# Quantised attention output transposed by DMA instead of TensorE, last four FFN tiles transposed by TensorE, all engine orders rewritten

## The reference, cut to what matters

```
x = layernorm(x + attn(x))              # attn: chunked recurrence with decay, W_write, W_read
# ffn, H = 256, I = 704:
xq = fp4_quant_dequant(x)               # per block of 16: scale = max|x|/6; q = grid(x/scale)*scale
gate = xq @ fp4_quant_dequant(w_gate).T
up   = xq @ fp4_quant_dequant(w_up).T
h    = silu(gate) * up
y    = fp4_quant_dequant(h) @ fp4_quant_dequant(w_down).T
out  = layernorm(x + y)
```

## Time and profile before

| | us |
|---|---|
| median of 3 runs | 320.72 (320.18 to 323.29) |
| the profiled execution | 319.53 |
| its span, first to last instruction | 317.8 |
| TensorE busy in the span | 299.8 (94%) |
| VectorE busy | 278.9 (88%) |
| GpSimd busy | 241.5 (76%) |
| ScalarE busy | 223.8 (70%) |

### The profile page before, as it was taken

How to read it: one execution, slowest core, us unless ns; L and a number is a source line. 1 busy time by engine, 2 the same in 40 slices (tenths; PEclk the granted TensorE clock), 3 DMA queues, 4 the chain that set the end, 5 groups by cost and what they waited for, 6 DMA issues and landing times.

```text
span 317.8 us, 6470 instructions
## 1 busy us (share of the span) xinstructions
PE 299.8 (94%) x1911; PEld 271.1 (85%) x1911; DVE 278.9 (88%) x725; ACT 223.8 (70%) x545; POOL 241.5 (76%) x258
## 2 busy tenths in 40 slices
PE   6949999999999989999999999999999999999783
PEld 2939988999899879889999998999999998899682
DVE  4996699969999999999988996989998899998953
ACT  7582986679677488669785886686877758587563
POOL 2897886476968967896978889487998757769671
PEclk9996999999999999999999999999999999999979
DMA  6704011832637446433562269338463273267601
GB/s 223 279 35 134 1 68 34 140 74 86 185 75 121 92 86 144 157 95 98 150 180 75 65 107 198 88 104 151 103 120 84 67 112 84 71 136 130 77 33 66
DMA packets 38722, 34.36 MB, mean 108 GB/s; under 512 B 25760, under 2 KB 31776, under 8 KB 38688
## 3 DMA queue, kind: packets, MB, share of 16 engines
q1 hardware_dynamic: 32064, 22.81, 34.5%
q10 hardware_dynamic: 6624, 11.15, 11.1%
HBM read 22.87 MB, written 5.18 MB: 88 GB/s over the span
## 4 chain that ended last, share of the span: by engine, by line
PE 67%; POOL 9%; issue 7%; DVE 7%; DMA 6%; ACT 3%; SPq 1%; ACTq 0%; POOLq 0%; DVEq 0%
PE ps L2160 15%; PE ps L2161 15%; PE ps L2164 15%; PE ps L2173 5%; PE ps L2174 5%; PE ps L2170 5%; DMA h_gT<-h_g 4%; POOL h_q L504 3%; DMA w_pair<-in_w_attn_dram 2%; PE ps L2224 2%; POOL h_n L485 1%; DVE hqT_lo L1584 1%; PE ps L2269 1%; POOL pr_lo L445 1%; PE ps L2283 1%
## 5 line engine op out<-in xcount | busy, mean ns | idle before, releaser
L2160 PE MATMUL ps<-guT_hi,xqT_hi 128*128 128x512 f32 (+1 forms) x192 | 74.0, 385 | 1.5 <-ACT xqT_hi L822 1.4
L2161 PE MATMUL ps<-guT_lo,xqT_hi 128*128 128x512 f32 (+1 forms) x192 | 72.1, 375 | 0.0
L504 POOL TENSOR_TENSOR h_q<-h_gT,h_sT 128x768 f32<-128x768 bf16 x30 | 51.8, 1731 | 12.3 <-DVE hqT_lo L1584 10.7
L2164 PE MATMUL ps<-guT_hi,xqT_lo 128*128 128x512 f32 (+1 forms) x192 | 56.5, 375 | 0.0
L485 POOL TENSOR_TENSOR h_n<-w_raw,h_rs 128x704 f32<-128x704 f32 x32 | 47.1, 1473 | 9.0 <-DVE h_rs L1414 8.9
L2160 PEld LDWEIGHTS ps<-guT_hi,xqT_hi 128*128 128x128 f32 x192 | 36.1, 188 | 6.8 <-ACT xqT_hi L822 1.7
L445 POOL TENSOR_TENSOR pr_lo<-pr,pr_hi 128x512 fp32r<-128x512 f32 (+3 forms) x32 | 28.5, 901 | 16.8 <-ACT pr_hi L791 16.8
L2164 PEld LDWEIGHTS ps<-guT_hi,xqT_lo 128*128 128x128 f32 x192 | 35.5, 188 | 6.0 <-DVE xqT_lo L1521 0.2
L2161 PEld LDWEIGHTS ps<-guT_lo,xqT_hi 128*128 128x128 f32 x192 | 36.1, 188 | 4.5
L2160 PE MATMUL ps<-dnT_hi,hqT_hi 128*128 128x256 f32 x160 | 39.6, 283 | 0.0
L2161 PE MATMUL ps<-dnT_lo,hqT_hi 128*128 128x256 f32 x160 | 39.5, 283 | 0.0
(11 more groups left out here) (130 smaller groups left out, 852.1 us busy)
## 6 DMA issues: line engine op xcount, KB each, us to landing
h_sT<-h_scales_dram SPq DMA_DIRECT2D x30, 384.0 KB
out_dram<-wq_gu ACTq DMA_DIRECT2D x31, 128.0 KB, 1.8
xs<-in_x_rows_dram ACTq DMA_DIRECT2D x7, 512.0 KB, 4.6
x_full<-in_xt_rows_dram ACTq DMA_DIRECT2D x6, 512.0 KB, 3.7
w_raw<-in_w_ffn_dram SPq DMA_DIRECT2D x6, 352.0 KB, 6.0
h_scales_dram<-h_s SPq DMA_DIRECT2D x30, 32.0 KB, 2.6
w_pair<-in_w_attn_dram SPq DMA_DIRECT2D x1, 512.0 KB, 5.1
x_full<-in_xt_rows_dram SPq DMA_DIRECT2D x1, 512.0 KB, 3.5
```

Source lines behind the costliest of these rows:

```text
L504: nc.gpsimd.tensor_tensor(h_q[:, p, :], h_gT[:, p, :, :].rearrange("p c t -> p (c t)"), h_sT[:, p, :], ALU.mult).then_inc(h_quant, 1)
L2160: nc.tensor.matmul(dst, lh, rh, start=(first and i == 0), stop=False)
L2161: nc.tensor.matmul(dst, lh, rl, start=False, stop=False)
L2164: last = nc.tensor.matmul(dst, ll, rh, start=False, stop=(end and i == len(terms) - 1))
```

## The change

- `xq_transpose` goes. `x_scale_rows` takes its place on TensorE: one small transpose of the scales (48 rows) per half batch. New are `copy_x_scales` on ScalarE and, on SyncE's queue, `write_x_scales`, `spread_x_scales` (256 KB) and `turn_x_grid` (a DMA transpose of 128x512 bf16), 16 of each.
- `x_dequant` becomes `x_spread`, which waits for both landings; `x_g` becomes bf16; `xq_round` and `xq_rest` read `x_q` from SBUF and no longer from PSUM.
- `x_divisors` writes the scales in the permuted layout that the transposed form wants.
- FFN tiles 28 and 29 leave the DMA path and go like 30 and 31: `h_dequant`, two `h_transpose` groups, `h_repeat`, `h_round`, `h_rest`. Their two sets of three DMAs and their `h_scale_rows` go.
- All tables of banks and all five orders are new. Between the two orders `gate_up(0)` moves behind both `reads` of batch 1, all `scores` and `values` of batch 2 and the weight fills 6 to 8; at the end `down(26)` moves ahead of `gate_up(31)`.

```diff
+            def write_x_scales(n, u):
+                sp.wait_ge(xs_copied, 2 * n + u + 1)
+                sp.dma_start(x_scales_dram[2 * n + u], x_s[:, u, :]).then_inc(xs_written[u], 16)
+            def spread_x_scales(n, u):
+                sp.wait_ge(xs_written[u], 16 * n + 16)
+                if n >= 1:
+                    sp.wait_ge(x_quant, 2 * n + u - 1)
+                sp.dma_start(x_sT[:, u, :], over_rows(x_scales_dram[2 * n + u], XC, 2 * DK)).then_inc(xs_landed[u], 16)
+            def turn_x_grid(n, u):
+                sp.wait_ge(x_grid, 2 * n + u + 1)
+                if n >= 1:
+                    sp.wait_ge(x_quant, 2 * n + u - 1)
+                sp.dma_start_transpose(x_gT[:, u, :, :], x_g[:, u, :]).then_inc(xg_turned[u], 16)
...
-            def x_dequant(n, u):
-                pool.wait_ge(x_grid, 2 * n + u + 1)
+            def x_spread(n, u):
+                pool.wait_ge(xs_landed[u], 16 * n + 16)
+                pool.wait_ge(xg_turned[u], 16 * n + 16)
                 if n >= 1:
-                    pool.wait_ge(xqT_filled, 2 * n + u - 1)
-                nc.gpsimd.tensor_tensor(
-                    blocks(x_q[:, 2 * u:2 * u + 2, :].rearrange("p i d -> p (i d)")), blocks(x_g[:, u, :]),
-                    per_block(x_ns[:, u, 0:2 * XB], 2 * XB), ALU.mult).then_inc(x_quant, 1)
+                    pool.wait_ge(xqT_lo_ready, 2 * n + u - 1)
+                nc.gpsimd.tensor_tensor(x_q[:, u, :], x_gT[:, u, :, :].rearrange("p c t -> p (c t)"), x_sT[:, u, :],
+                                        ALU.mult).then_inc(x_quant, 1)
...
+            def copy_x_scales(n, u):
+                act.wait_ge(xs_filled, 2 * n + u + 1)
+                if n >= 1:
+                    act.wait_ge(xs_written[u], 16 * n)
+                nc.scalar.copy(x_s[:, u, :], ps[0:XHELD, xs_at[n][u], 0:P]).then_inc(xs_copied, 1)
...
             def x_to_grid(n, u):
+                if n >= 1:
+                    dve.wait_ge(xg_turned[u], 16 * n)
                 to_grid(x_g[:, u, :], ps[:, x_sq_at[n][u], :], x_y[:, u, :], x_magic, x_grid, 2 * n + u + 1)
...
             def xq_rest(n, u):
                 dve.wait_ge(xqT_hi_ready, 2 * n + u + 1)
-                c = slice(D * u, D * (u + 1))
-                nc.vector.tensor_tensor(xqT_lo[:, :, c], ps[:, xq_at[n][u], :].rearrange("p (c t) -> p c t", c=DK),
-                                        xqT_hi[:, :, c].bitcast(F32), ALU.subtract).then_inc(xqT_lo_ready, 1)
+                c = slice(2 * u, 2 * u + 2)
+                nc.vector.tensor_tensor(xqT_lo[:, c, :, :].rearrange("p i c t -> p (i c t)"), x_q[:, u, :],
+                                        xqT_hi[:, c, :, :].rearrange("p i c t -> p (i c t)").bitcast(F32),
+                                        ALU.subtract).then_inc(xqT_lo_ready, 1)
...
-            def xq_transpose(n, u, free):
-                pe.wait_ge(x_quant, 2 * n + u + 1)
+            def x_scale_rows(n, u, free):
+                pe.wait_ge(x_div, 2 * n + u + 1)
                 wait_all(free)
-                for dk in range(DK):
-                    for q in range(2):
-                        at = dk * 2 * P + q * P
-                        last = nc.tensor.matmul(ps[:, xq_at[n][u], at:at + P], x_q[:, 2 * u + q, dk * P:(dk + 1) * P], ident[:],
-                                                is_transpose=True, start=(dk == 0 and q == 0),
-                                                stop=(dk == DK - 1 and q == 1))
-                last.then_inc(xqT_filled, 1)
+                nc.tensor.transpose(ps[0:XHELD, xs_at[n][u], 0:P],
+                                    x_ns[:, u, :], ident[:]).then_inc(xs_filled, 1)
```

More of the change, by code:

```diff
@@ L565, in _ @@
-            x_stats(2, 0)
             p_rest(2, 2)
             p_rest(2, 3)
-            x_rest(3, 0)
-            x_rest(3, 1)
+            x_stats(2, 0)
+            x_spread(1, 0)
+            h_normalise(0, 0)
             x_normalise(2, 0)
+            x_stats(2, 1)
+            h_normalise(1, 1)
+            x_spread(1, 1)
+            h_normalise(2, 0)
+            p_rest(3, 0)
+            h_normalise(3, 1)
+            h_spread(0, 0, 1)
+            p_rest(3, 1)
+            x_spread(2, 0)
@@ L600, in _ @@
-            h_normalise(10, 0)
-            p_rest(4, 0)
-            x_stats(3, 1)
+            x_spread(2, 1)
+            h_normalise(7, 1)
+            out_stats(0, 0)
+            out_stats(1, 1)
+            h_spread(4, 0, 3)
+            x_stats(3, 1)
+            h_spread(5, 1, 3)
+            p_rest(4, 0)
+            h_normalise(8, 0)
+            p_rest(4, 1)
+            x_normalise(3, 1)
+            h_normalise(9, 1)
+            h_spread(6, 0, 4)
+            h_spread(7, 1, 4)
+            out_stats(2, 0)
@@ L603, in _ @@
+            x_spread(3, 0)
+            x_stats(4, 0)
+            p_rest(4, 2)
+            x_rest(5, 0)
+            p_rest(4, 3)
+            h_normalise(10, 0)
+            x_normalise(4, 0)
+            h_normalise(11, 1)
+            out_stats(3, 1)
+            x_rest(5, 1)
+            x_spread(3, 1)
+            x_stats(4, 1)
             h_spread(8, 0, 5)
+            h_normalise(12, 0)
             out_stats(4, 0)
-            h_spread(9, 1, 5)
-            h_normalise(11, 1)
-            p_rest(4, 1)
@@ L626, in _ @@
-            x_normalise(4, 1)
             p_rest(5, 0)
             p_rest(5, 1)
+            h_spread(9, 1, 5)
+            x_normalise(4, 1)
+            h_normalise(13, 1)
+            x_spread(4, 0)
+            out_stats(5, 1)
+            out_stats(6, 0)
+            h_spread(10, 0, 6)
+            x_stats(5, 0)
+            h_spread(11, 1, 6)
+            p_rest(5, 2)
+            out_stats(7, 1)
+            x_rest(6, 0)
+            p_rest(5, 3)
+            x_normalise(5, 0)
+            x_rest(6, 1)
@@ L678, in _ @@
+            h_normalise(19, 1)
+            out_stats(12, 0)
             p_rest(7, 0)
             x_normalise(6, 1)
[L680 to L692 removed]
@@ L693, in _ @@
-            x_dequant(7, 0)
+            p_rest(7, 1)
+            out_stats(13, 1)
+            x_spread(6, 0)
+            h_normalise(20, 0)
+            x_stats(7, 0)
+            h_normalise(21, 1)
+            x_normalise(7, 0)
+            out_stats(14, 0)
+            x_spread(6, 1)
+            h_spread(18, 0, 10)
+            out_stats(15, 1)
+            h_normalise(22, 0)
+            h_spread(19, 1, 10)
+            h_normalise(23, 1)
+            out_stats(16, 0)
+            p_rest(7, 2)
@@ L694, in _ @@
+            h_spread(20, 0, 11)
+            p_rest(7, 3)
+            h_spread(21, 1, 11)
+            h_normalise(24, 0)
+            h_normalise(25, 1)
+            h_spread(22, 0, 12)
+            x_stats(7, 1)
+            out_stats(17, 1)
+            out_stats(18, 0)
+            x_spread(7, 0)
+            x_normalise(7, 1)
+            h_spread(23, 1, 12)
+            out_stats(19, 1)
+            h_normalise(26, 0)
             h_spread(24, 0, 13)
-            x_stats(7, 1)
             out_stats(20, 0)
-            h_normalise(26, 0)
```

2295 lines of the change are left out of this document (1148 added, 1147 removed).

## The result

| | median of the runs | ratio to the kernel before |
|---|---|---|
| before | 320.40 us (318.56 to 323.29, 20 runs) | 1 |
| after | 321.35 us (319.34 to 324.69, 20 runs) | 1.0052, interval 1.0027 to 1.0077 |

A forecast was written before the change was run, and what follows sets the result against it. TensorE was taken to bound the long middle, VectorE close behind, with a chain in the tail. 319.5 - 2.9 (middle) - 4.0 (tail) + 0 (start) + 1.5 (VectorE) = 314.1, adjusted from profile to median: 314.8 us; range 310.5 to 322.

The forecast's parts named there:

- TensorE's sum, -4.0 us: Attention transposes removed, -7.0; scale transposes, +1.8 and -0.2; transposes of FFN tiles 28 and 29, +1.4: -4.0 us.
- The tail, -4.0: Behind the last `gate_up`: 24.5 us before, 20.0 at the best after; -4.0 us taken, ends -5 and -1.
- The start, 0: Up to the first `gate_up`, near 49 us: GpSimd decides, TensorE's lead is given back; 0, ends -5 and +2.
- Hidden: Work costed at nothing: `copy_x_scales` on ScalarE (4.1 us), `x_spread` on GpSimd, 48 more and 6 fewer DMAs on SyncE.
- VectorE, +1.0 us of work: 16 subtractions `xq_rest` with both inputs in SBUF, 745 ns against 682; TensorE's gaps in the middle +1.5, ends 0 and +3.
- VectorE bounds the middle: Rival, chance 0.20: VectorE can't exceed 92.5% in the middle, TensorE's gain there is lost, only the tail's remains: 316.5 us.
- GpSimd's line stands for landings: Rival, chance 0.16, slower: 44 multiplications in GpSimd's line wait for DMAs; at 1.5 us mean lateness, 327 us.
- The signs: Whole span: TensorE busy near 296, last `gate_up` ending 290 to 291, subtraction near 745 ns; wrong if middle idle exceeds 5 us.

The follow-up runs named there:

- b_eight_transposes: The kernel before with each group of four xq transposes done twice: 326.34 us, 1.0191 of the kernel before.
- b_tail: The kernel before with only the new tail: FFN tiles 28 and 29 transposed by TensorE, last orders rewritten: 321.94 us, 1.0027 of the kernel before.
- a_turn_first: The changed kernel with tile 14's transpose moved ahead of the two spreads in SyncE's list (the swap): 316.68 us, 0.9886 of the kernel before.
- the third buffer: The changed kernel with three instead of two buffers for the grid values h_g: 314.55 us, 0.979 of the kernel before; run again, 0.9834.
- the second result: The changed kernel with three h_g buffers, run again in the third set: 316.41 us, 0.9834 of the kernel before.

## Why the prediction was wrong, step by step

- **TensorE's sum, -4.0 us**: right. The instructions are as counted (L2224 gone), and b_eight_transposes shows that a group's 0.44 us is paid.
- **The tail, -4.0**: right in size, 24.5 to 19.9, and no DMA is in its chain. Of the reason only part is shown (b_tail gained nothing).
- **The start, 0**: right, and much as described. The first `gate_up` stands at 49.46, and TensorE's surplus ahead of it is 14.2 us against 14.3. Between 17 and 31 us TensorE was busy 13.15 of 14 us at a granted clock of 1.00, where it had been 9.90 at 0.76; then it stood 1.7 us for a weight tile of GpSimd at 36.2 us. Up to 17 us the granted clock was 0.90 instead of 1.00, which was not forecast.
- **Hidden: this step failed.** It costed the 42 net DMAs, and the new order of SyncE's queue, at nothing, except for what waits in GpSimd's line and in SyncE's. It did write that "what waits in it holds the FFN's transposes behind", and did not ask who waits for a transpose besides the dequantisation. Two do: GpSimd reads what it wrote, and VectorE waits until it has read. What the runs showed in its place: tile 14's transpose, behind two spreads, landed after 10.13 us, VectorE stood 4.06 us for it and TensorE 3.18. Rows had the distance: a landing of 8.9 us at the longest and two buffers. Price by a_turn_first: 1.0052 - 0.9886 = 1.7%, 5.3 us; by the third buffer 2.2 to 2.6%, 7.0 to 8.4 us. The intervals of the swap and of the second result overlap, those of the swap and of the first just miss each other. Between forecast and median lie 6.5 us, so this step alone accounts for most or all of it: with the third buffer the kernel stands at 0.979 to 0.9834 of 320.4, which is 313.7 to 315.1 us, where 314.8 was forecast.
- **VectorE, +1.0 us of work, entered in the sum as +1.5 us of gaps: the work was mis-sized.** It grew by 5.4 us. Its price is seen three ways, none of them sharp: 2.9 us for 2.7 of work in the kernel before (by the profile of its fastest execution), 3.8 for 6.4 in the changed one, 1.6 of 4.9 with three buffers, within the noise. For 4.4 us more than forecast that would be an estimated 1.5 to 4 us. Since the kernel with the third buffer stands at the forecast all the same, either something else gave that back or little of it was paid; no run tells. The working scaled L1584's mean (1118 for 768 columns) down by columns, but the part of it that is collision does not shrink with the columns of the one that waits. Six in 16 were held up, for 0.9 us more each; the 1.90 us one above began 0.03 us behind a GpSimd instruction of 1.38 us and ended 0.55 us behind its end. The Trainium skill, SBUF — State Buffer, section "Who interferes with whom", calls the ports that the two engines share an exclusive lock, and says that the order of issue decides who blocks. The trace agrees: those held up were the ones that began second. By these six, the price of one that is held up is about what remains of GpSimd's instruction when it begins.
- **The rivals.** "VectorE bounds the middle" (0.20) came nearest in its reason and gave 316.5, where the changed kernel without its landing wait took 314.55 to 316.68; the runs neither bear it out nor rule it out. "GpSimd's line stands for landings" (0.16) had the right cause, long landings, at the wrong engine: GpSimd waited 0.8 us for one in all, VectorE 5.0. Its price, 314.8 + 13 = 327.8 (the prediction has 327), was built on an average lateness over 44 waits; what happened was one landing, at one place.
- **The signs.** The prediction named 5 us of TensorE's idle time between the first and the last `gate_up` as a sign that it is wrong; it is 5.7 us (248.90 - 243.16). The last `gate_up` ends at 298.4, not 290 to 291, TensorE's busy time is 299.2, not near 296, and the subtraction averages 1016 ns, not 745.
- **The measured 321.35 is within the range of 310.5 to 322**, by its slow end only, and that is luck: the range went so far up for the sake of the GpSimd case. The time moved up and not down. Its ratio is within 1%, to which the prediction gave 0.23.

## What to carry to other kernels

For every transfer, list its two ends: who waits for what it writes, and who waits until it has read. The second wait is silent while there is room, and a longer landing goes straight into the engine that refills the buffer. Where an order is rewritten, look in the issuing queue for large transfers bunched ahead of one that somebody needs; moving one line was worth 1.7% here, and another buffer 2.2 to 2.6%. And cost an instruction with two SBUF inputs by how many meet GpSimd and for how long, not by scaling a mean.

## What the runs showed of the hardware, unexpected

- A transpose of 192 KB, issued at nearly the same moment, landed after 10.13 us behind two spreads of 384 KB, and after 5.3 us ahead of them. Behind them it took 7.1 to 10.1 us in ten traces, ahead of them 4.1 to 5.3 in three. Spreads are not the only way to a long landing: the 8.9 us of the earlier trace rows stood behind one spread only, with a 512 KB load from ScalarE's queue issued 0.3 us ahead of it, which itself took 8.0 us. No run parts the two.
- The issue of a transpose can be slow too: the second one behind the two spreads held SyncE's queue for 2.77 us in the changed kernel, the first 1.26. A transpose in flight is not enough for that: in a_turn_first tile 14's took 1.23 us to issue while x's was in flight.
- A VectorE instruction with an input from PSUM was never held up by GpSimd (at most 693 ns in 16), the same one with both inputs in SBUF was in 6 of 16 (up to 2195 ns), and one with a single input in SBUF was too (up to 1892 ns).
- More work on an engine can cost nothing, or less: 5.3 us added to TensorE, with 0.9957 against 1.0052.
